# VectorE's product buffer and both column masks held in PSUM during the gather passes of a graph network

## The reference

```python
h = jnp.maximum(_layernorm(x, axis=-1), 0.0)
x = x + _L0_gnn_ref(h, ...)      # one segment_sum over the edges
...
x = x + _L1_gnn_ref(h, ...)      # edge filters, one segment_sum
...
x = x + _L2_gnn_ref(h, ...)      # four EdgeConv layers, a segment_max each
...
x = x + _L3_gnn_ref(h, ...)      # two GCN layers, a segment_sum each
```

## Time and profile before

| | |
|---|---|
| median of 3 runs | 10542.4 us (10541.9 to 10545.94) |
| span of the profiled execution | 10630.0 us |
| GpSimd busy | 8032.4 us, 76% |
| VectorE busy | 4419.4 us, 42% |
| TensorE busy | 1639.5 us, 15% |
| ScalarE busy | 543.8 us, 5% |
| 5824 gathers of the seven passes (L991) | 6249.0 us |

### The profile page before, as it was taken

One profiled execution on the slowest core, in us unless ns is written; L12 is line 12 of the kernel. 1 busy time (PEld: TensorE's weight loads), 2 busy tenths in 40 slices (PEclk: granted clock), 3 DMA queues, 4 the chain that ended last, 5 costly groups with the idle time before them and its releaser, 6 DMA issues. The chain is left out here.

```text
span 10630.0 us, 49732 instructions
## 1 busy us (share of the span) xinstructions
PE 1639.5 (15%) x9025; PEld 1437.8 (14%) x9025; DVE 4419.4 (42%) x9272; ACT 543.8 (5%) x1417; POOL 8032.4 (76%) x7137
## 2 busy tenths in 40 slices
PE   2000048888860000100001000100001000010000
PEld 1000047777750000100001000100001000010000
DVE  4444434444443444344443444334444444444444
ACT  2000021111130000000000000000001000000000
POOL 4777768888847777677776777777777777777777
PEclk7555567777775555555555555555555555555555
DMA  5444435555532333333333333323333333333333
GB/s 190 142 142 142 145 88 77 77 74 76 77 86 91 95 95 95 99 95 95 95 97 97 95 95 95 101 93 95 95 95 98 96 95 95 95 100 95 95 95 104
DMA packets 467313, 1064.01 MB, mean 100 GB/s; under 512 B 156534, under 2 KB 276192, under 8 KB 412586
## 3 DMA queue, kind: packets, MB, share of 16 engines
q0 software_dynamic: 320736, 464.07, 19.8%
q1 hardware_dynamic: 143480, 597.45, 15.5%
q10 hardware_dynamic: 2940, 1.00, 0.0%
HBM read 517.80 MB, written 552.72 MB: 101 GB/s over the span
## 5 line engine op out<-in xcount | busy, mean ns | idle before, releaser
L991 POOL DMA_INDIRECT WORK<-table,S x5824 | 6249.0, 1073 | 2037.5 <-issue 1772.7
L1045 DVE TENSOR_TENSOR Z<-WORK,RESET 128x512 f32<-128x512 f32 x612 | 423.5, 692 | 2615.7 <-DMA WORK<-table,S 2601.8
L1210 POOL DMA_INDIRECT acc<-TOT,stage x832 | 1300.8, 1564 | 276.0 <-issue 207.6
L1090 PE MATMUL bank<-ident,WORK 128*128 128x128 f32 x7 | 3.3, 474 | 8069.6 <-DVE WORK L1074 8069.6
L1045 DVE TENSOR_TENSOR Z<-WORK,KEEP 128x512 f32<-128x512 f32 x459 | 317.6, 692 | 1958.9 <-DMA WORK<-table,S 1948.5
L1090 PEld LDWEIGHTS bank<-ident,WORK 128*128 128x128 f32 x7 | 1.3, 183 | 8071.1 <-DVE WORK L1074 8071.1
L1048 DVE TENSOR_TENSOR WORK<-WORK,Z 128x512 f32<-128x512 f32 x1071 | 741.0, 692 | 36.5
L1064 DVE TENSOR_TENSOR WORK<-WORK,Z 128x1536 f32<-128x1536 f32 (+2 forms) x448 | 633.8, 1431 | 12.4
L1059 DVE TENSOR_TENSOR Z<-WORK,S 128x1536 f32<-128x1536 f32 (+2 forms) x448 | 633.6, 1431 | 12.3
L1415 DVE SCALAR_TENSOR_TENSOR BASE<-bank,WEIGHT,BASE 128x128 f32<-128x128 f32 x832 | 234.2, 344 | 839.8 <-PE bank L1285 772.3
L1053 DVE SCALAR_TENSOR_TENSOR WORK<-WORK,S 128x128 f32<-128x128 f32 x1428 | 502.5, 352 | 50.9
(11 more groups left out here) (247 smaller groups left out, 2663.4 us busy)
## 6 DMA issues: line engine op xcount, KB each, us to landing
run_rows<-WORK SPq DMA_DIRECT2D x357, 1024.0 KB, 4.1
WORK<-table,S POOLq DMA_INDIRECT x5824
fill_rows<-BASE SPq DMA_DIRECT2D x52, 1024.0 KB, 6.8
WORK<-fill_rows SPq DMA_DIRECT2D x104, 512.0 KB
table<-TF SPq DMA_DIRECT2D x56, 384.0 KB
WORK<-carry_rows SPq DMA_DIRECT2D x49, 384.0 KB
acc<-TOT,stage POOLq DMA_INDIRECT x832
acc<-Z SPq DMA_DIRECT2D x12, 1024.0 KB
```

Of the source, the lines that this page charges most:

```text
L991: pool.indirect_dma_start(RING_T[:, b * WIDE + k, :], None, table, table_row(table, INDEX[:, t:t + 1]))\
L1045: step(dve.tensor_tensor(TMP[:, 0:groups, 0, :], rows[:, :, j - 1, :], mask(keep[:, :, j], groups, 0), op0))
L1210: pool.indirect_dma_start(acc_dram[a], bass.IndirectOffsetOnAxis(stage[:, h, j % HALF:j % HALF + 1].bitcast(u32), 0), TOT[:, j // QUAD % 2 ...
```

## The change

The product buffer `TMP` moves from SBUF (`Z`) to PSUM banks 5 to 7, with one bank for each of its three columns of a group. At the head of each pass VectorE copies both column masks to PSUM (banks 1 to 4, from column 256 of bank 1 on): the `keep` mask (`KEEP` or `RESET`) and `PREFIX`, 832 columns each. The `tensor_tensor` instructions of `combine` read the masks and `TMP` there. The `scalar_tensor_tensor` of L1053 keep the scalar from `PREFIX` in SBUF, and both their tensor inputs are rows of the ring in SBUF as before; L1074 is not touched. The four PSUM tensors become one of eight banks so that a view can run over several.

```diff
-        TMP = Z[:, 0:3 * GROUPS * F].rearrange("p (g j f) -> p g j f", g=GROUPS, j=3)
...
-        banks = [ctx.enter_context(nc.psum_tensor(f"bank{i}", [P, 1024], f32)) for i in range(4)]
+        banks = ctx.enter_context(nc.psum_tensor("bank", [P, 4096], f32))
+        MASKS = banks[:, 512 + 256:512 + 256 + 2 * T].rearrange("p (k t) -> p k t", k=2)
+        TMP = banks[:, 5 * 512:8 * 512].rearrange("p (j g f) -> p g j f", j=3, g=GROUPS)
...
         def bank(i, n=1):
-            return banks[i // 2][:, i % 2 * 512:(i % 2 + n) * 512]
+            return banks[:, i * 512:(i + n) * 512]
...
                 if masks is not None:
                     prefix_masks(dve, st, masks)
+                st.did(dve.tensor_copy(MASKS[:, 0, :], scale[:]))
+                st.then(dve.tensor_copy(MASKS[:, 1, :], PREFIX))
                 n = 0
...
-                    keep = scale[:, t0:t0 + FOUR * groups].rearrange("p (g j) -> p g j", j=FOUR)
-                    prefix = PREFIX[:, t0:t0 + FOUR * groups].rearrange("p (g j) -> p g j", j=FOUR)
+                    keep, prefix = (MASKS[:, k, t0:t0 + FOUR * groups].rearrange("p (g j) -> p g j", j=FOUR)
+                                    for k in range(2))
...
                         step(dve.scalar_tensor_tensor(RING_T[:, last, :], RING_T[:, (last - FOUR) % SPAN, :],
-                                                      prefix[:, g, FOUR - 1:FOUR], RING_T[:, last, :], op0, op1))
+                                                      PREFIX[:, t0 + FOUR * g + FOUR - 1:t0 + FOUR * g + FOUR],
+                                                      RING_T[:, last, :], op0, op1))
```

## The result

The changed kernel takes 9793.12 us (median of 4 runs, 9789.99 to 9795.05) against 10542.15 us: a ratio of 0.9289, 95% interval [0.9276, 0.9302]. The forecast was 9798.

The account below looks back on a forecast made before the run. The prediction took GpSimd's gathers and the pauses between them to bound the kernel. Its terms, -748 (`tensor_tensor`) + 4 (carries) + 0 (copies) = -744 us, took 10542.4 to 9798 us; range 9770 to 9870.

Parts of the forecast that it names:

- The bound: In the seven gather passes, only GpSimd's gathers and the pauses between them set the time, about 1146 us a pass.
- The four kinds of `tensor_tensor`: Per chunk, masked products and combinations would have one SBUF input, so stretched gathers fall to 0.944 us: 748 us saved.
- The carries: Four single-column `scalar_tensor_tensor` of a chunk keep two SBUF inputs and hold gathers only in their last part: 4 us lost.
- The rival of the carries: Reads fall in the last part of one or two carries per chunk: +46 to +93 us, 9840 to 9890; chance 0.08.
- The copies: Two mask copies at each pass head, 1.2 to 2.1 us a pass, hidden while VectorE idles: counted as 0 us.
- VectorE's speed: A `tensor_tensor` with a PSUM input takes 681 to 692 ns, from SBUF 692: no difference; writing PSUM not shown.
- What is late next: In the passes DMA share rises from 0.30 to 0.33, first pass 0.42 to 0.46; GpSimd stays the bound.
- The median from the span: Trace span 10630.0 becomes 9886; the median lies 87.6 us below the span, giving 9798 us.
- The lower end: If the 87.6 us are recording cost, 12 ns per GpSimd instruction, stretched gathers give back up to 21 us more: 9777.
- No change: In the passes, any long enough `tensor_tensor` could hold gathers: 10,542 to 10,556 with the copies; chance 0.03.
- the half: In a chunk, L1059 alone, with its output in PSUM, goes on holding gathers: some 310 us back, 10,110; chance 0.03.
- VectorE as the bound: In the passes, PSUM access slows VectorE's `tensor_tensor` so GpSimd waits for `reduced`: at 3 times, +1000, 11,540; chance 0.03.

Follow-up runs that it names:

- the first two runs: The changed kernel with only the product buffer in PSUM, masks in SBUF: 10,239.35 us; with only the masks in PSUM, product buffer in SBUF: 10,427.67 us.

## Why the prediction was right, and where it wasn't

**The bound** was read rightly: pauses and waits of the gathers are what they were, and GpSimd still waits for nothing else in a pass.

**The four kinds of `tensor_tensor`**: 748 us forecast, 749.2 measured (6249.0 less 5499.8). That they agree to 1 us is luck: the gathers of two executions of the kernel before differ by 10 us. That the number of SBUF inputs makes the difference was argued from two neighbouring gathers. One reading there was wrong: the row of L1169 is two instructions, and the one at work when the gather needed its read ended at 9337.60, so a held gather would have lasted 1.27 us, not 1.60; at 0.94 it was free all the same. The halves of the change, the exchanged operands and the products issued twice now show the difference for each kind, for either output and, in L1051 and L1068, for either place.

**The carries**: 4 us forecast; the trace after has 17 stretched gathers under L1056 with 1.8 us in all. I had put the read at the edge of the second carry's held part, from a chunk that starts 0.16 us after a gather. The median chunk starts 0.23 after one, so the read comes 0.14 us into the carry, clear of the part from 0.22 on. The rival of the carries was priced at 46 to 93 us; with the reads moved into the held part it came to 22.

**The copies**: 1.2 to 2.1 us a pass forecast, 1.03 and 1.02 us measured, hidden as said; the gathers beside them were not held.

**VectorE's speed**: no difference was forecast for reads, and there is next to none. For 512 elements the halves of the change keep the two apart: a mask from PSUM saves 5 ns (687 against 692 with the output in SBUF), an output in PSUM, which no row had shown, costs 8 to 9 (700 against 692 with the masks in SBUF, 696 against 687 with them in PSUM). The 9.45 us of an uncut chunk are 9.41 by their own terms, which changes nothing.

**What is late next**: DMA share 0.33 and 0.46, as forecast.

**The median from the span**: the step was wrong, though its result was not. I let the 87.6 us stay in the trace and so expected a span of 9886; it is 9793.2. They belonged to one execution, outside the passes. The step did no harm because both sides were formed without them. The lower end, 9777, which took them for a cost of recording, had no ground.

**The rivals.** No change, the half and VectorE as the bound didn't come. The half was priced wrongly: 357 x 0.9 is 321, not 310, and, more to the point, a gather under L1059 alone would not keep its old stretch. With the product buffer alone in PSUM nearly all of the stretch is under that one instruction, and it is 449 us, so the rival should have read about 10,240 and not 10,110. The ground for "no change", that `tensor_tensor` would not stall a DMA of GpSimd, falls with the first two runs: here it does, by up to 1.6 us.

## What to carry to other kernels

Where GpSimd issues indirect DMAs back to back, look at the spread of their durations, not only at the idle times: a mean well above the minimum says that something holds some of them, and a constant offset from the end of a VectorE instruction names it. Where PSUM has room, give a `tensor_tensor` at most one SBUF input, and put the output of a copy or the input of a `tensor_scalar` there; in the changed kernel a `tensor_tensor` takes as long as before to 5 ns, while in the experiments the copy took 1.8 and the `tensor_scalar` 1.7 times as long. Move all of them: with one half moved, the next holding instruction catches the same gather, and shares booked to instructions in a trace don't add.

## What was not expected of the hardware

The masks alone gave back 117 of 749 us, the product buffer alone 302: the stretch depends on which instruction a gather's read meets next.

Nor does a carry hold over its whole length. In the changed kernel a carry lasts 0.352 us, and the gathers are stretched only where their read, reckoned at 0.12 us after the gather's start, falls 0.22 us or more after the carry's start (17 gathers). Where it falls at 0.15 to 0.22 us (142 gathers) the gather takes its usual 0.94 us and it is the carry that lasts longer, up to 0.42 us. So each can wait for the other, and it looks as if the first to come has its way; that is inferred from these durations. When the carries were moved by a quarter of a microsecond, their cost went from 1.8 to some 22 us.
